# One wait per gather instead of a stop every eight, in layers two and three of a graph network

## The reference, cut to what matters

```python
# layer two: x_src is gathered by the edge's source, expanded by 8 coefficients, summed by target
x_src = node_feat[src]
xb = jnp.einsum('ei,bio->ebo', x_src, weight)
coef = w_comp[edge_type]
msg = jnp.einsum('ebo,eb->eo', xb, coef)
msg = msg * in_norm[dst]
agg = jax.ops.segment_sum(msg, dst, num_segments=N)
...
# layer three: h is gathered by the source, scaled, summed by target
h = x @ weight
out = jax.ops.segment_sum(h[row] * norm[:, None], col, num_segments=n)
```

## Time and profile before

| | us |
|---|---|
| median of three executions | 23,802.61 |
| lowest and highest | 23,789.50 and 23,813.24 |
| the profiled execution | 24,039.33 |
| its span | 24,037.5 |

### The profile page before, as it was taken

How to read it: one execution, slowest core, us unless ns; L and a number is a source line. 1 busy time by engine, 2 the same in 40 slices (tenths; PEclk the granted TensorE clock), 3 DMA queues, 4 the chain that set the end, 5 groups by cost and what they waited for, 6 DMA issues and landing times. The chain is left out here.

```text
span 24037.5 us, 205919 instructions
## 1 busy us (share of the span) xinstructions
PE 10326.4 (43%) x47565; PEld 6860.3 (29%) x47566; DVE 16546.3 (69%) x26071; ACT 2139.0 (9%) x3670; POOL 12605.7 (52%) x12782
## 2 busy tenths in 40 slices
PE   0033326655555555556666422222333333333333
PEld 0033322222222222222222322222333332333332
DVE  8744439988888888886666211115888886878887
ACT  0011110000000000000000000001111111111111
POOL 0188876655566555536665166653444443444443
PEclk9999997555555555558887555555555555555555
DMA  4133331111111111121112001113111112111112
GB/s 170 25 69 69 69 64 25 24 23 23 22 21 23 23 23 23 22 20 24 24 24 23 9 21 21 21 21 49 52 51 50 51 50 41 52 51 50 52 50 42
DMA packets 1118452, 942.42 MB, mean 39 GB/s; under 512 B 775931, under 2 KB 887579, under 8 KB 1117875
## 3 DMA queue, kind: packets, MB, share of 16 engines
q0 software_dynamic: 419904, 437.84, 9.9%
q1 hardware_dynamic: 698096, 500.67, 8.0%
HBM read 726.46 MB, written 207.32 MB: 39 GB/s over the span
## 5 line engine op out<-in xcount | busy, mean ns | idle before, releaser
L1420 POOL DMA_INDIRECT tail<-ball,h_idx x3328 | 3271.7, 983 | 1793.3 <-issue 1231.1
L736 PE MATMUL p_rad<-w_stack,hid_t 99*128 99x512 bf16 (+1 forms) x6656 | 3079.6, 620 | 2391.3 <-DVEq L826 1161.0
L808 DVE TENSOR_REDUCE red<-prod 128x96 f32<-128x1536 f32 x1664 | 2898.3, 1742 | 3.5
L1098 POOL DMA_INDIRECT l_xg<-h_tab,l_idx x1664 | 1571.2, 944 | 1444.1 <-issue 828.3
L1452 PE MATMUL h_sum<-head,h_hot 128*128 128x64 f32 x6656 | 1444.2, 421 | 1987.4 <-ACT head L1498 1987.4
L1438 PE MATMUL h_head<-ball_parts,hot_t 128*128 x9984 | 1067.6, 281 | 2813.4 <-issue 1578.1
L337 POOL DMA_INDIRECT rec_a<-rec,slot x1600 | 1990.4, 1244 | 517.2 <-issue 500.5
L692 POOL DMA_INDIRECT rec_b<-l_rcb x1600 | 1920.0, 1200 | 571.6 <-issue 570.5
L930 POOL DMA_INDIRECT l_xg<-x_tab,l_idx x1664 | 1571.6, 944 | 1141.8 <-issue 874.0
L946 PE MATMUL l_sum<-outer,l_hot 128*128 128x512 f32 x3328 | 1693.3, 673 | 945.6 <-DVEq L991 869.7
L736 PEld LDWEIGHTS p_rad<-w_stack,hid_t 99*128 99x128 bf16 (+1 forms) x6656 | 774.5, 132 | 4337.7 <-issue 4336.0
(11 more groups left out here) (369 smaller groups left out, 18896.7 us busy)
## 6 DMA issues: line engine op xcount, KB each, us to landing
hot_t<-rows_l SPq DMA_DIRECT2D x208, 512.0 KB
rec_a<-fill SPq DMA_DIRECT2D x128, 728.0 KB, 19.6
l_rec<-rec_a SPq DMA_DIRECT2D x104, 896.0 KB, 4.8
rhot_t<-rows_r SPq DMA_DIRECT2D x208, 384.0 KB
tail<-ball,h_idx POOLq DMA_INDIRECT x3328
t<-in_type SPq DMA_DIRECT2D x100, 500.0 KB
l_xg<-in_x,l_idx POOLq DMA_INDIRECT x1664
l_xg<-x_tab,l_idx POOLq DMA_INDIRECT x1664
```

The costliest lines, as they stand in the source:

```text
L736: ins = pe.matmul(p_rad[j % 2][:, h * 512:(h + 1) * 512], hid_t[j // 4 % 2][0:K3 + 3 * (1 - i), j % 4, i, :], w_stack[i][0:K3 + 3 * (1 - i ...
L808: ch.step(dve.tensor_reduce(red[:, j, :], prod[j % 3][:, :, :], AX, ALU.add))
L1420: pool.indirect_dma_start(tg[q][:, j, :], None, table[:, :], bass.IndirectOffsetOnAxis(ap=idx[q][:, j:j + 1], axis=0)).then_inc(gathered[q ...
```

## The change

The stop after every eighth gather goes, in both layers. Each gather now has a wait of its own ahead of it: for the gather four before it. The semaphores `gathered[0]` to `gathered[3]` no longer belong to a buffer each; gather j of a block adds to `gathered[j % 4]`. Since a block has 16 gathers, gather j and gather j - 4 share a semaphore, also across blocks, and the count to wait for is `(it * 4 + u) * (4 * BT) + 16 * (j // 4)`. The first four gathers of a layer have none to wait for, so the first pass of the loop is written out ahead of it and the loop runs from 1. The users of a block (DVE in layer two, PE in layer three) wait for all four semaphores instead of one. The buffers, the indices, `idx_ready` and the number of gathers stay.

```diff
         @block.gpsimd
         def _(pool):
-            with pool.Fori(0, NB // 4) as it:
+            def gathers(it, first):
                 for u in range(4):
                     hold(pool, turn, idx_ready, it * 4 + (u + 1))
                     for j in range(BT):
+                        if not first or u or j >= 4:
+                            hold(pool, turn, gathered[j % 4], (it * 4 + u) * (4 * BT) + 16 * (j // 4))
                         pool.indirect_dma_start(xg[u][:, j, :], None, table[:, :],
-                                                bass.IndirectOffsetOnAxis(ap=idx[u][:, j:j + 1], axis=0)).then_inc(gathered[u], 16)
-                        if j % 8 == 7:
-                            hold(pool, turn, gathered[u], it * (16 * BT) + 16 * (j + 1))
+                                                bass.IndirectOffsetOnAxis(ap=idx[u][:, j:j + 1], axis=0)).then_inc(gathered[j % 4], 16)
+
+            gathers(0, True)
+            with pool.Fori(1, NB // 4) as it:
+                gathers(it, False)
...
-                dve.wait_ge(gathered[u], it * (16 * BT) + 16 * BT)
+                for k in range(4):
+                    dve.wait_ge(gathered[k], (it * 4 + u) * (4 * BT) + 4 * BT)
...
                     hold(pe, turn, hot_done, b + 1)
-                    hold(pe, turn, gathered[u], it * (16 * BT) + 16 * BT)
+                    for k in range(4):
+                        hold(pe, turn, gathered[k], b * (4 * BT) + 4 * BT)
                     hold(pe, turn, added, b + 1)
```

## The result

**The changed kernel took 23,945 us (median of 4 runs) where the kernel before took 23,808: ratio 1.0057, 95% interval 1.004 to 1.0075.** The forecast was 22,994, a ratio of 0.966. It was wrong, and of the other sign. Its saving and its ratio nevertheless come back in a later comparison of the same two kernels: 22,748 against 23,546 us, ratio 0.966 (0.9644 to 0.9677). Its time doesn't, since there the kernel before was faster too. Most of what follows is about what differs between the two comparisons.

A forecast was written before the change was run, and what follows sets the result against it. No engine bound throughout; POOL's program, half work and half waiting for landings, set the pace in layers two and three. Layer three -463 and layer two -346 make -809 us, from 23,802.6 to 22,994 us; range 22,830 to 23,170.

The forecast's parts named there:

- The pitch: POOL, layers two and three: gathers stay 1.249 us apart, since landings come 1.37 us before they are needed.
- the bounds, zero to 0.05 us: POOL's new waits: price per hold taken as zero, bad end 0.05 us each (83 us a layer).
- Rival (c): POOL: a hold can't pass until the gather before is done; pitch 2.11 us, 25,690 us in all; chance 0.04.
- Rival (b): Gathers without pause land slower: at 5.5 us landing-to-restart, 534 us saved, 23,269 us; chance 0.10.
- DVE's own block is longer: Layer two: DVE needs 20.63 us a block without waiting, against POOL's 20.0, so DVE binds; 21.4 with turns.
- sums of the stops: POOL's stops cost 487 us in layer three and 496 us in layer two, 2.35 and 2.39 us each.
- some 13: Layer three: PE would wait some 13 us a block after the change.
- The padding blocks: Layer three's last three blocks: slow landings, 1.75 us each, leave 24 us of the stops not won.
- The turn: DVE between layer two's blocks: 0.40 us idle plus 0.24 for three more waits remain.
- the loop's turn: Layer two, DVE: the loop's turn every fourth block adds 0.10 us a block, bound 0.33.
- PE's slow restart: Layer two: PE restarts at its lower clock, so DVE's 1.5 us wait after its third `outer` stays.
- rival (a): Layer two: PE stays at 2.4 GHz, DVE's 1.5 us goes, POOL binds; 950 us saved, 22,853 us; chance 0.08.

The follow-up runs named there:

- e4: The changed kernel, all its waits kept, with a full stop on all four semaphores put back after every eighth gather: 23,803 us, ratio 0.9989.
- h1: The changed kernel itself, unaltered, timed again in a later comparison against the kernel before at 23,546 us: 22,748 us, ratio 0.966.
- h3: Same kernel as e1 (no stops or landing waits), timed again beside a kernel before of 23,546 us: 22,757 us, ratio 0.9665.
- h2: The kernel before, stops kept, with 80 semaphore instructions per block added on DVE in layer three (trace shows 40): 23,528 us.
- i1: Same kernel as h2, run once more in another comparison beside a kernel before of 23,547 us: 23,521 us.
- i2: e1 with gathers of layers two and three fetching 128-byte rows in place of 256 (wrong rows, half the data left out): 22,595 us.
- e1: The kernel before with the stop every eight gathers taken out and no wait for landings on POOL: 23,918 us, ratio 1.0034.
- f4: Layer three as in the changed kernel, layer two as in the kernel before: 23,665 us, ratio 0.9928 against the kernel before.
- E and F: Two follow-up comparisons of kernels with stops, waits or look-ups varied; the kernel before took 23,830 and 23,831 us beside them.
- G, H and I: Three later comparisons, of new variants and repeats of earlier kernels; the kernel before took 23,546 or 23,547 us beside them.

## Why the prediction was wrong, point by point

**POOL: right, in both conditions.** The pitch stayed 1.25 us, gaps 0.30, holds free. e4 prices the waits at zero within its interval; h1 against h3 has layer three 17 us longer, and some 15 of them are waits in the padding blocks; the median pitch is 1.249 us in both, and the mean of all pitches under 1.6 us is 3 ns longer. Layer two is 30 us longer, but there DVE and not POOL sets the pace. The whole kernel is equal (22,748 and 22,757). That is inside the bounds, zero to 0.05 us. The Trainium skill's picture ("Perfetto Trace Analysis", section on the SWDGE DMA instruction) of a sequencer that goes on while the instruction waits in its queue agrees with the trace: such waits were passed while a gather was running. Rival (c) is out.

**Rival (b), slower landings, is out** in the blocks where it mattered: 2.1 us from start to landing with or without stops. In form it came nearest, since its 23,269 us was the one price for "something doesn't bear gathers without a pause"; it had the wrong thing, and still priced it as a gain of 534 us where 137 were lost.

**The step that failed** is the one that isn't written as a step: "DVE's own block is longer ... 20.63 us a block", and that PE's and DVE's instructions would come at the same pace when POOL no longer pauses. I took DVE's block from a trace in which POOL paused 2.4 us after every eighth gather and carried it over to one in which it doesn't. In the condition of the first comparison it doesn't carry: the block became (13,302.7 - 10,429.8) / 104 = 27.6 us in place of 21.4, and in layer three PE and DVE, with 17 us of slack, used up all of it. The forecast had 0.94 on faster, and no rival in which the engines that are waited for get slower through POOL's pace. A reader of the trace of before could have had one: register additions of 639 ns stand beside others of 45. The "issue" of 2,115 us at an engine that plainly waits for PE was a sign too, but of a trace that lacks increments. The prediction's sums of the stops took "issue" and landings together and aren't hurt by it. Why the pace falls, by records or otherwise, stays open.

**Without the condition, the sum holds.** The comparison is h1 with the kernel before at 23,546, whose layers I take from h2 and i1 (layer two unchanged there, layer three with added increments that cost nothing).

| | forecast | measured |
|---|---|---|
| layer three | -463, to 2,102 us | 2,093 us; 2,581 - 2,093: -488 |
| layer two | -346, to 2,221 us | 2,272 us; 2,588 - 2,272: -316 |
| in all | -809 | -798 (ratio 0.966) |

That the two totals are 11 us apart is partly luck: layer three gave 25 us more than was said and layer two 30 us less. The time itself, 22,748 us, lies below the range of 22,830 to 23,170 even so, since the kernel before was 257 us below the 23,803 that the forecast started from.

*Layer three.* PE waits for gathers 1,389.1 us, 13.4 a block, where "some 13" was said:

```profile
PE l_sum L1122 <- DMA l_xg<-h_tab,l_idx: 1389.1, 104, 38.7
```

The padding blocks: pauses of mostly 0.5 to 1.2 us come back there, and from 15,096.05 to 15,117.70 thirteen pitches take 21.65 us, 1.67 us each; the term was 1.75. The layer's 2,093 us are 16 above the 2,077 of 1,663 undisturbed pitches, so the padding cost 16 us of the 24. The stops were worth 2,581 - 2,077 = 504 us there in place of 487.

*Layer two.* DVE's turn between blocks, in h1:

```profile
12002.28 1.23 DVE L986 TENSOR_TENSOR outer<-l_pcoef,l_xg 128x1024 f32<-128x1024 f32 x1 [0.58 <-DMA l_xg<-x_tab,l_idx]
...
12023.17 1.23 DVE L986 TENSOR_TENSOR outer<-l_pcoef,l_xg 128x1024 f32<-128x1024 f32 x1 [0.58 <-DMA l_xg<-x_tab,l_idx]
...
12069.67 1.22 DVE L986 TENSOR_TENSOR outer<-l_pcoef,l_xg 128x1024 f32<-128x1024 f32 x1 [5.81 <-DMA l_xg<-x_tab,l_idx]
```

The turn is 0.58 us (0.40 + 0.24 was said) and the block 20.89 us, as before. The term that was mis-sized is the loop's turn: every fourth block DVE stands still for 5.8 us and the block takes 25.7, in place of 0.10 us a block (bound 0.33). (25.7 - 20.9) / 4 = 1.2 us a block. In the trace three instruction packets of 8 KB arrive just then (12,065.2 to 12,070.6), so it looks like DVE's or PE's next instructions being fetched, though the profile puts the wait down to the gathers. i2 bears it out: its layer two, the same loop with half rows, has 4 such packets where h3's has 125, and its fourth block takes 21.0 us. (Why it fetches nothing is not known.) The packets lay in the trace of before as well (126), under POOL's stops. It costs some 25 x 4.8 = 120 us. The other three blocks of four take 20.7 to 21.4 us, less than the 21.4 of the sum, so the mean is 22.07 (2,273 us over 103 blocks): 0.67 us or 69 us too little forecast. Against the kernel before the miss is only 30, since its own layer two is 15 us longer without the condition (2,588 against 2,574) and the layer's two ends are counted with the gathers. PE's slow restart (DVE's 1.5 us wait after its third `outer`) is still there, so rival (a) is out: DVE basis_sums in h1 (the fourth operation of the block)

```profile
12007.95 0.69 DVE L977 TENSOR_TENSOR basis_sums<-basis_sums,l_sum 128x512 f32 x1 [1.50 <-PE l_sum L950]
```

**Which kernel is best** depends on the condition too. Without it the change itself and e1/h3 are, at 22,748 and 22,757 us (3.4% below). With it f4, 0.7% below, is, and the change loses 0.6%. A kernel with f4's layers was not run without the condition; as an estimate from the table it would have layer two at about 2,588 and layer three at 2,093, some 23,060 us, still 2% below the one before.

## What to carry to other kernels

Before an engine's pauses are taken away, look at what the others do in them: here, under the condition, DVE and PE kept their pace only with POOL's pauses, so durations read beside them did not hold without them. Two marks could be read before the change was made: register additions that take 0.6 us beside others of 45 ns, and fewer increments of a semaphore in the trace than its DMAs make. The second says that the trace itself is incomplete, and that the recording may be part of what is measured. "Issue" idle at an engine that in truth waits for another can come of it, but is no mark by itself: POOL's stops stand under "issue" in h2 too, whose increments are all but complete. And a change of a few per cent is worth timing in more than one comparison: here it was 0.6% slower in one and 3.4% faster in another, each with an interval of about a sixth of a per cent to either side.

## What the runs showed of the hardware

- In comparisons E and F and the first one, DVE's and PE's instructions came one per 0.70 or 1.40 us (a matmul with its weight load 2.80 us) some time after POOL had begun to issue gathers at a pitch of 1.25 us without a pause (in e1 7.6 us at the earliest, in layer three); pauses of 2.7 us after eight gathers kept it away but for 4 to 6 us in all, 1.4 us did so in part. In G, H and I the same kernels never showed it.
- The amount of instructions that DVE got through before that was 48 to 54 in layer two of e1, whether it took 11.2 or 18.9 us, and 36 to 46 in layer three.
- In the same comparisons the traces lack semaphore increments: 5,488 of 26,624 of layer three's gathers are in the changed kernel's, 26,624 in h1's. Instruction packets are equal in number in both whole traces (431 on queue 14), and six in the slow layer three.
- Landings (2.0 to 2.2 us after a gather's start) and POOL's own pace didn't notice.
- A gather's rows of 128 bytes in place of 256 cost the same on POOL (layer three 2,079 and 2,076 us, where h3 had 2,076); layer two became 150 us shorter than h3's (2,093 against 2,242), and with it went the instruction packets of the loop (4 against 125).
- A semaphore wait and increment that is met before POOL reaches it cost at most 3 ns of the gathers' pitch (layer three of h1 against h3: median 1.249 us in both, mean of all pitches under 1.6 us 1.252 against 1.249).
- Where layer two's loop turned, every fourth block, DVE stood still for 5.8 us in h1 while three instruction packets of 8 KB came.
